# Relation maxima in a two-layer GNN kernel: where the begin rows are issued, how deep they are buffered, and where the accumulators are cleared

## What is computed

```python
es = jnp.einsum('nhd,hd->nh', x, a_s)
ed = jnp.einsum('nhd,hd->nh', x, a_d)
logit = jax.nn.leaky_relu(es[src] + ed[dst], NEG_SLOPE)
logit = jnp.where(mask[:, None], logit, -1e+30)
mx = jax.ops.segment_max(logit, dst, num_segments=N)
mx = jnp.maximum(mx, -1e+30)
p = jnp.exp(logit - mx[dst]) * mask[:, None]
den = jax.ops.segment_sum(p, dst, num_segments=N)
alpha = p / jnp.where(den > 0, den, 1.0)[dst]
msg = alpha[..., None] * x[src]
out = jax.ops.segment_sum(msg, dst, num_segments=N)
```

## Time and profile before

| | |
|---|---|
| median of 3 runs | 5955.15 us (5943.6 to 5958.23) |
| the profiled execution | 5968.85 us |
| its span, first to last instruction | 5967.0 us |
| TensorE busy | 3616.4 us (61%) |
| VectorE busy | 3898.3 us (65%) |
| GpSimd busy | 3782.6 us (63%) |
| ScalarE busy | 1442.3 us (24%) |
| gathers of relation_maxima, L725 | 832, 786.1 us busy, 710.9 us idle before them |
| scans, L763 | 103, 240.3 us busy, 335.4 us idle before them |
| granted TensorE clock, mean | 0.758 |

### The profile page before, as it was taken

One profiled execution on the slowest core, in us unless ns is written; L12 is line 12 of the kernel. 1 busy time (PEld: TensorE's weight loads), 2 busy tenths in 40 slices (PEclk: granted clock), 3 DMA queues, 4 the chain that ended last, 5 costly groups with the idle time before them and its releaser, 6 DMA issues. The chain is left out here.

```text
span 5967.0 us, 110677 instructions
## 1 busy us (share of the span) xinstructions
PE 3616.4 (61%) x18587; PEld 2574.6 (43%) x18588; DVE 3898.3 (65%) x11908; ACT 1442.3 (24%) x3070; POOL 3782.6 (63%) x3803
## 2 busy tenths in 40 slices
PE   0153333333314777771558788788778787888877
PEld 0122222222214666661425555555555455555546
DVE  4644444444427666668947777777777777777774
ACT  0120000000004555553332222222222222222222
POOL 3136655565555777765217788888887788878770
PEclk9875565555555555555679999998999999899899
DMA  2254444444423555543157788888887888888874
GB/s 54 62 159 116 111 113 109 114 116 114 108 66 98 130 129 130 130 119 110 47 161 172 173 178 183 178 182 175 180 178 174 179 180 179 179 178 179 178 153 136
DMA packets 895552, 836.72 MB, mean 140 GB/s; under 512 B 228060, under 2 KB 752636, under 8 KB 895257
## 3 DMA queue, kind: packets, MB, share of 16 engines
q0 software_dynamic: 217200, 396.10, 32.2%
q1 hardware_dynamic: 641257, 406.10, 25.1%
q10 hardware_dynamic: 37008, 33.70, 2.4%
HBM read 597.83 MB, written 237.64 MB: 140 GB/s over the span
## 5 line engine op out<-in xcount | busy, mean ns | idle before, releaser
L1543 POOL DMA_INDIRECT sums<-msg_bsum,k_sidx x831 | 1323.3, 1592 | 303.3 <-issue 261.4
L725 POOL DMA_INDIRECT max_xe<-rows,max_idx x832 | 786.1, 945 | 710.9 <-ACT max_idx L797 401.8
L1678 PEld LDWEIGHTS msg_both_ps<-msg_onehot,msg_hid 128*128 128x128 f32 x3712 | 562.4, 208 | 1222.4 <-issue 832.0
L1557 POOL DMA_INDIRECT msg_ga<-ab,k_bsrc x832 | 826.0, 993 | 369.9 <-issue 200.6
L1691 PE MATMUL msg_pre_ps<-msg_rw,msg_lt 128*128 128x512 f32 x1856 | 1047.7, 648 | 8.8 <-DMA msg_rw<-ab 8.8
L1643 ACT ACTIVATE msg_low_ps<-msg_xs 128x512 f32<-128x512 f32 x928 | 558.1, 601 | 2012.7 <-DVE msg_xs L1612 1033.3
L1678 PE MATMUL msg_both_ps<-msg_onehot,msg_hid 128*128 128x64 f32 x3712 | 616.0, 292 | 520.4 <-DVE msg_bsum L1587 338.8
L956 POOL TENSOR_SCALAR att_keyhot<-k_ramp,att_keys 128x128 f32<-128x128 f32 x1028 | 611.6, 611 | 276.2 <-ACT att_keys L1028 276.2
L1611 DVE TENSOR_TENSOR msg_xs<-msg_pre_ps,msg_ga 128x256 f32<-128x256 f32 x928 | 390.8, 421 | 532.1 <-PE msg_pre_ps L1691 219.5
L1622 DVE TENSOR_TENSOR msg_hid<-msg_xs,msg_low_ps 128x512 f32<-128x512 f32 x928 | 637.0, 686 | 106.4 <-issue 40.2
L1068 PE MATMUL att_sum_ps<-att_px,att_keyhot 128*128 128x136 f32 x2056 | 559.0, 453 | 220.5 <-DVE att_px L990 215.3
(11 more groups left out here) (296 smaller groups left out, 6031.3 us busy)
## 6 DMA issues: line engine op xcount, KB each, us to landing
msg_rw<-ab SPq DMA_DIRECT2D x928, 128.0 KB
l_outside<-xe SPq DMA_DIRECT2D x1028, 72.0 KB, 2.5
xe<-max_xe SPq DMA_DIRECT2D x104, 576.0 KB
att_keyrow<-key ACTq DMA_DIRECT2D x257, 128.0 KB, 3.3
msg_lt<-in_efT SPq DMA_DIRECT2D x928, 32.0 KB
rows<-node_rows SPq DMA_DIRECT2D x50, 288.0 KB, 2.4
max_begin<-begin SPq DMA_DIRECT2D x104, 128.0 KB
max_xe<-rows,max_idx POOLq DMA_INDIRECT x832
```

The source lines that it names most:

```text
L725: pool.indirect_dma_start(xe[:, b, u, :], None, T.rows, bass.IndirectOffsetOnAxis(ap=idx[:, b, u:u + 1], axis=0)).then_inc(s_xe[b], 16)
L1543: pool.indirect_dma_start(T.sums[k % 2], bass.IndirectOffsetOnAxis(ap=K.sidx[:, k:k + 1], axis=0), bsum[:, (k + 1) % SB, :], None, compute ...
L1557: pool.indirect_dma_start(ga[:, (k + 1) % RB, :], None, T.ab, bass.IndirectOffsetOnAxis(ap=K.bsrc[:, k:k + 1], axis=0)).then_inc(s_ga[k % ...
L1678: pe.matmul(fwd_ps[u % 2][:, q * WIN:(q + 1) * WIN], hid[:, b % 2, u, HID + q * P:HID + (q + 1) * P], onehot[:, b, u, :], start=True, stop ...
```

## The change

Four edits. (1) `begins` moves from SyncE to ScalarE, as the last step of a tick there, and its buffer and semaphores go from two to four. It now waits for the scan four groups earlier instead of two. (2) hl and `parts` go; TensorE reads halves directly, at a column that in the loop is given by a register. (3) acc is no longer cleared in relation_maxima but in node_maxima, behind the copy on line 881 and before the wait for the gathers. (4) acc is allocated after relation_maxima.

```diff
-        begin = ph.sb("begin", [RH, 2, G * P])
+        begin = ph.sb("begin", [RH, RG, G * P])
...
-        s_beg = [ph.sem(f"beg{b}") for b in range(2)]
+        s_beg = [ph.sem(f"beg{b}") for b in range(RG)]
...
-            def begins(j, b):
-                if past(j, 2):
-                    sp.wait_ge(s_scan, j - 1)
-                sp.dma_start(begin[:, b % 2, :], T.begin[ds(j, 1), :].to_broadcast([RH, G * P])).then_inc(s_beg[b % 2], 16)
...
-            pipeline(sp, GROUPS, RG, [(0, begins), (1, store_rows), (3, store_runs)])
+            pipeline(sp, GROUPS, RG, [(1, store_rows), (3, store_runs)])
...
-            L.mark(dve.memset(srcf[:, BLOCKS:NB], -1.0))
-            L.link(dve.memset(acc[:, :, :], 0.0))
+            L.link(dve.memset(srcf[:, BLOCKS:NB], -1.0))
...
-                dve.wait_ge(s_beg[b % 2], filled(j, b, 2, 16) if isinstance(j, int) else (j - b % 2) * 8 + 16)
+                dve.wait_ge(s_beg[b], filled(j, b, RG, 16))
...
-            def parts(j, b):
-                if past(j, 2):
-                    dve.wait_ge(s_src, (j - 1) * 2)
-                dve.tensor_copy(hl[:, b % 2, :, :], halves[:, ds(j * G, G), :]).then_inc(s_hl, 1)
...
-            pipeline(dve, GROUPS, RG, [(2, scan), (0, parts), (1, separate), (2, firsts)])
+            pipeline(dve, GROUPS, RG, [(2, scan), (1, separate), (2, firsts)])
...
+            def begins(j, b):
+                if past(j, RG):
+                    act.wait_ge(s_scan, j - RG + 1)
+                    settle(act, K)
+                act.dma_start(begin[:, b, :], T.begin[ds(j, 1), :].to_broadcast([RH, G * P])).then_inc(s_beg[b], 16)
...
-            pipeline(act, GROUPS, RG, [(0, indices), (3, move_back)])
+            pipeline(act, GROUPS, RG, [(0, indices), (3, move_back), (0, begins)])
...
             def sources(j, b):
-                pe.wait_ge(s_hl, j + 1)
...
-                        pe.matmul(src_ps[q][:, u, :], hl[:, b % 2, v, 0:1].to_broadcast([P, P]), K.identb128[:, :],
+                        pe.matmul(src_ps[q][:, u, :], halves[:, ds(j * G + v, 1), 0].to_broadcast([P, P]), K.identb128[:, :],
...
             L.mark(dve.tensor_copy(both[:, :, :, 0, :], ed4))
+            L.mark(dve.memset(acc[:, :, :], 0.0))
             dve.wait_ge(s_run, 16 * TILES)
```

More of the change, by code:

```diff
@@ L660, in _, with relation_maxima @@
             pipeline(pe, TILES, 2, [(0, transpose), (1, products)])
-def relation_maxima(nc, K, T, acc):
+def relation_maxima(nc, K, T):
     with Phase(nc, "max") as ph:
@@ L677, in relation_maxima @@
         real = ph.sb("real", [P, 1])
-        hl = ph.sb("hl", [P, 2, G, 2], BF16)
         junk = ph.sb("junk", [P, G, P], BF16)
@@ L687, in relation_maxima @@
         s_rst = [ph.sem(f"rst{b}") for b in range(RG)]
-        s_beg = [ph.sem(f"beg{b}") for b in range(2)]
-        s_idx, s_m, s_tr, s_scan, s_bk, s_rt, s_hl, s_src, s_dup = (
-            ph.sem(n) for n in ("idx", "m", "tr", "scan", "bk", "rt", "hl", "src", "dup"))
+        s_beg = [ph.sem(f"beg{b}") for b in range(RG)]
+        s_idx, s_m, s_tr, s_scan, s_bk, s_rt, s_src, s_dup = (
+            ph.sem(n) for n in ("idx", "m", "tr", "scan", "bk", "rt", "src", "dup"))
         block = ph.block()
@@ L762, in scan @@
                 first = isinstance(j, int) and j == 0
-                dve.tensor_tensor_scan(run[:, b % 2, :], begin[:, b % 2, :], mT_ps[b % 2][:, :],
+                dve.tensor_tensor_scan(run[:, b % 2, :], begin[:, b, :], mT_ps[b % 2][:, :],
                                        -BIG if first else run[:, 1 - b % 2, G * P - 1:G * P],
                                        ALU.add, ALU.max).then_inc(s_scan, 1)
-            def parts(j, b):
-                if past(j, 2):
-                    dve.wait_ge(s_src, (j - 1) * 2)
-                dve.tensor_copy(hl[:, b % 2, :, :], halves[:, ds(j * G, G), :]).then_inc(s_hl, 1)
             def firsts(j, b):
@@ L834, in sources @@
                         v = q * G // 2 + u
-                        pe.matmul(src_ps[q][:, u, :], hl[:, b % 2, v, 0:1].to_broadcast([P, P]), K.identb128[:, :],
+                        pe.matmul(src_ps[q][:, u, :], halves[:, ds(j * G + v, 1), 0].to_broadcast([P, P]), K.identb128[:, :],
                                   start=True, stop=False)
-                        last = pe.matmul(src_ps[q][:, u, :], hl[:, b % 2, v, 1:2].to_broadcast([P, P]), K.identb[:, :],
+                        last = pe.matmul(src_ps[q][:, u, :], halves[:, ds(j * G + v, 1), 1].to_broadcast([P, P]), K.identb[:, :],
                                          start=False, stop=True)
@@ L841, in _, with node_maxima @@
             pipeline(pe, GROUPS, RG, [(2, back), (1, transpose), (1, sources)])
-def node_maxima(nc, K, T):
+def node_maxima(nc, K, T, acc):
     with Phase(nc, "top") as ph:
@@ L1876, in build @@
             node_inputs(nc, K, T)
+            relation_maxima(nc, K, T)
             acc = l0.sb("acc", [P, KSLOTS, XR])
-            relation_maxima(nc, K, T, acc)
             with Phase(nc, "l0a") as l0a:
@@ L1881, in build @@
                 K.edm = l0a.sb("edm", [P, KSLOTS, TERMS * 2 * H], BF16)
-                node_maxima(nc, K, T)
+                node_maxima(nc, K, T, acc)
                 relation_attention(nc, K, T, acc)
```

## The result

The changed kernel takes 5997.8 us (median of 5 runs, 5972.8 to 6000.82) where the kernel before takes 5955.15 (5 runs in the same comparison, 5923.55 to 5958.23): ratio 1.0074, 95% interval 1.0041 to 1.0107. It is slower by some 44 us, more than the 0.3% that a measurement tells. 5923 was forecast, faster; the sign was wrong. The time is near that of rival 3 at its dearest (5994), but only in part by its mechanism.

A forecast was written before the change was run, and what follows sets the result against it. The prediction took GpSimd's gathers as the floor (1040 us), with 267.9 us of pauses above. -6 - 4 - 44 + 22 = -32 us; 5968.85 - 32 - 13.7 = 5923 us, range 5810 to 6000 (forecast's own 5895 to 5945).

The forecast's parts named there:

- rival 3: relation_maxima: pause pattern stays and ScalarE's issue sits in every pause; +12 us, or 5994 us at 0.9 each; chance 0.24.
- +22 for ScalarE's issue: ScalarE, between copy-back and index copy: the begin issue adds 0.40 us to each of 54 GpSimd pauses, +22 us.
- 5.5 becoming 4.6: Transposes of m would start 4.6 instead of 5.5 us after gathers resume, VectorE 0.5 sooner and gathers 0.4 later.
- -44 for the long pauses: relation_maxima without hl: GpSimd's 13 long pauses shrink to 4.8 us, 13 x 3.4 = -44 us.
- the rule of the prediction: Transposes starting 4.1 us after gathers resume let the scan run amid gathers; at 5.5 they are held to the end.
- -4 for m: separate on VectorE ahead of the wait for products: 12 pauses ending with m lose 0.3 us each, -4 us.
- -6 for the memset: Start of relation_maxima: without the accumulators' memset, GpSimd's first pause of 6.05 us goes, -6 us.
- The bound of 0: Bound of the memset's gain: 0 if TensorE's signals are held in the first pause too.
- Four buffers 0: Two begin buffers becoming four: no scan waits for its begin row and nobody for the stores, 0 us.
- register instructions 0: TensorE, 16 register instructions more per group: covered by the scan of 2.33 us, 0; without cover 52 us.
- node_maxima 0: The memset moved to node_maxima fits VectorE's idle 64.54 us there and costs 0.
- rival 4: node_maxima: the memset slows the gathers, at most by its 22.7 us, 5978 us; chance 0.02.

The follow-up runs named there:

- begins_first: The changed kernel with ScalarE issuing the begin row ahead of the copy-back instead of behind it: 5944.9 us, ratio 1.0003 to the kernel before.
- hl_only: The kernel before with only hl and parts removed, products read by register address: 5932.4 us, ratio 0.998 to the kernel before.
- acc_only: The kernel before with only acc allocated after relation_maxima and cleared in node_maxima: 5944.32 us, ratio 0.9998 to the kernel before.
- pad_pe: The kernel before with 64 semaphore increments on TensorE behind the loop of relation_maxima: 5661.55 us, ratio 1.0013 to the kernel before.
- pad_dve: The changed kernel with 17 semaphore increments on VectorE behind the loop of relation_maxima: 5974.97 us, ratio 1.005 to the kernel before.
- begins_first_2: begins_first run again in a later comparison: 5953.66 us, ratio 1.0009 to the kernel before.
- hl_pad_2: The kernel before with the edit on hl and 17 semaphore increments on VectorE behind the loop, second comparison: 5927.92 us against 5950.16, ratio 0.9961.

## Why the prediction was wrong

- **+22 for ScalarE's issue.** The place (every pause for the index copy runs through it) and the 0.40 us per pause were right: short pauses grew from 4.56 to 4.95 us. The effect was not a sum of such delays. The changed kernel against begins_first gives 42 us instead of 22, a bare delay of 0.51 us 57 us instead of 26. What is missing goes together with the long pauses, which the delay brings back (12 instead of 4, 20 instead of 7). This is the step that failed: the forecast added -44 and +22 as if independent, and even let the 0.4 us of delay help the hold (5.5 becoming 4.6), with a threshold drawn from two rows.
- **-44 for the long pauses.** Alone, with the padding, the edit on hl gives 0.39%, 23 us (interval 15 to 31, the 4 for m among them); in hl_only nine of 13 long pauses go. Its sign was right and its size about twice too large. Its reason falls in part. I count the stretches of 16 gathers without a pause of over 1 us inside, by when the first transposes of m start. In the kernel before, the scan runs amid the gathers where they start up to 4.98 us after the gathers resume, and in all 13 cases from 5.09 us on it waits for the gathers to end: so far the rule of the prediction. But in the changed kernel all 12 cases at 4.62 to 4.64 us are held and those up to 4.30 are not, so the limit is not a fixed distance. (In hl_only it is not even sharp: of six cases at 5.04 to 5.63 us two pass just before the gathers end.) And in hl_only the eight transposes that start 5.0 us after are held as well; there GpSimd stops after eight gathers, and the pause is a short one:

```profile
1049.69 0.94 POOL L724 DMA_INDIRECT max_xe<-rows,max_idx  x1 [4.57 <-ACT max_idx L791]
...
1054.72 1.89 PE L809 MATMUL max_mT_ps<-k_ident,max_m 128*32 128x128 f32 x8
...
1061.42 2.33 DVE L762 TENSOR_TENSOR_SCAN max_run<-max_begin,max_run,max_mT_ps 32x1024 f32<-32x1024 f32 x1 [4.04 <-remote]
...
1062.40 0.94 POOL L724 DMA_INDIRECT max_xe<-rows,max_idx  x1 [3.03 <-ACT max_idx L791]
```

The last gather ended at 1059.37, and the scan came 2.05 us later. A ninth, also 5.04 us after but with 16 gathers running, was held 17.79 us before a pause of 8.19. hl_only has 14 pauses after only eight gathers, the kernel before four, the changed kernel none. So the edit on hl removed long pauses in good part by another pattern of stops, which the prediction did not have; what decides between the patterns stays open.
- **-4 for m.** The waits for m are gone, but the pauses now end with the index copy. No saving of its own can be seen. (Beside the 54 pauses that the prediction counted there are 15 of 1.6 to 1.9 us, which the trace puts down to issue; "nearly all others are 3.0 to 4.9" passes over them.)
- **-6 for the memset.** 0 (acc_only 0.9998; first pause 6.55 there and 6.83 in the changed kernel, against 6.05). The bound of 0 was the right one, for the reason given there: pad_pe, with the memset in its old place but without the hold, has no such pause.
- **Four buffers 0, register instructions 0, node_maxima 0.** Four buffers and node_maxima: right, and rival 4 did not happen. The register instructions were not measured alone; they are part of the edit on hl.
- **What no step had: +13 us in relation_attention.** The prediction looked only for costs in the stages that the diff touches. Without it the change would still be slower (pad_dve, 1.005).
- **The sum again.** Measured apart from the changed kernel are -23 for the edit on hl and +13 for VectorE's code. The delay of 0.51 us cost 57; scaled to 0.39 us that is 44 (my estimate). Together +34, where 44 was measured, with an interval of 24 to 64. Rival 3 had the right place, but its mechanism was the length of the issue alone: it reached 5994 by 0.9 us per pause for an issue that cost 0.4.

A profile of one execution leaves some 17 us open in this stage (begins_first 1287.1 and begins_first_2 1304.6 us are the same kernel), so single stage lengths here back the ratios and don't replace them.

## What to carry to other kernels

Where an engine's pause repeats in a pattern, a delay inside it is not priced by its own length: test it as a bare delay before adding it to a gain that rests on the same pattern. A DMA issue moved to an idle engine belongs where that engine waits anyway, ahead of the step that others wait for, not behind it (begins_first against the change, 42 us here). And when a stage that was not edited changes its time by an equal amount per loop pass, pad the program of the engine whose code got shorter or longer before looking for contention. And a limit drawn from two rows is to be counted over the whole stage, in more than one kernel, before a term rests on it.

## What the runs showed of the hardware

- The hold on TensorE's signals is there in some comparisons only, and then in every kernel of it: the same kernel before took 5955, 5944, 5949 and 5950 us in four comparisons, 6026 in one, and 5655 in two. In the changed kernel the gathers need 1038 us where there is no hold and 1333 where there is.
- Without it a copy-back follows the start of its transposes by 0.77 us (1003.18 to 1003.95); with it by 10.9 us in the earlier trace rows (1025.92 to 1036.83).
- With it, the first transposes of m after the gathers resume still pass amid 16 gathers in a row if they start early enough: up to 4.98 us in the kernel before, up to 4.30 in the changed kernel. From 5.09 and 4.62 us on they are held to the end of the gathers.
- 17 instructions executed once on VectorE, with no work in them, shorten a later stage by 13 us (852.1 to 839.3 us, pad_dve against the changed kernel; hl_pad_2 840.0 against hl_only's 851.7); 64 on TensorE cost their own 6 to 7 us and leave that stage at 839.3.
- A memset of 22.73 us on VectorE leaves the gathers beside it at 1.25 us each (1764.88 to 1766.13).
